# Gather loop of a graph and mixture kernel: in its last 254 tiles each product waits for the tile before it, and four loops of the sort written out

## What is computed

```python
xn = _layernorm(x, axis=-1)
# graph: 100000 edges; edge_row = src, edge_col = dst (nodes), edge_val = weight
gathered = edge_val[:, None] * xn[edge_col]
agg = jax.ops.segment_sum(gathered, edge_row, num_segments=N_NODES)
x = x + einsum('nd,od->no', agg, W) + b + linear_attention(xn)
# then two of eight experts for each node
x = x + ffn(_layernorm(x))
```

## Time and profile before

| | us |
|---|---|
| median of 3 runs | 2421.96 (2420.9 to 2422.66) |
| the profiled execution, its own time | 2401.91 |
| its span, first to last instruction | 2400.1 |
| sort: POOL's indirect DMAs, first to last | 117.2 to 304.4 |
| gather loop: POOL's first gather to the last add | 324.4 to 1656.9 |
| of it tiles 648 to 901, first to last add | 1298.3 to 1656.9 |

### The profile page before, as it was taken

One profiled execution on the slowest core, in us unless ns is written; L12 is line 12 of the kernel. 1 busy time (PEld: TensorE's weight loads), 2 busy tenths in 40 slices (PEclk: granted clock), 3 DMA queues, 4 the chain that ended last, 5 costly groups with the idle time before them and its releaser, 6 DMA issues. The chain is left out here.

```text
span 2400.1 us, 48331 instructions
## 1 busy us (share of the span) xinstructions
PE 1626.9 (68%) x13448; PEld 1218.7 (51%) x13448; DVE 1423.3 (59%) x3495; ACT 1317.3 (55%) x4250; POOL 1388.1 (58%) x1333
## 2 busy tenths in 40 slices
PE   6877435666666566666564444344549999999998
PEld 3565424454544455455452222222347777777776
DVE  7998535555556565555565555556845555555555
ACT  6455335555555555555555555554556565656555
POOL 3688846666666666666666666665404444444443
PEclk8898868888887788888886565655559999999999
DMA  4022144444444443333333333433512223232222
GB/s 147 14 84 75 58 127 136 133 134 136 136 134 131 130 123 101 104 103 102 104 91 90 93 110 116 154 123 98 173 31 44 50 47 50 45 51 47 48 48 32
DMA packets 139656, 225.26 MB, mean 94 GB/s; under 512 B 33398, under 2 KB 94016, under 8 KB 139298
## 3 DMA queue, kind: packets, MB, share of 16 engines
q0 software_dynamic: 67040, 146.22, 23.5%
q1 hardware_dynamic: 66022, 69.75, 9.2%
q10 hardware_dynamic: 6364, 6.40, 0.8%
HBM read 181.40 MB, written 41.82 MB: 93 GB/s over the span
## 5 line engine op out<-in xcount | busy, mean ns | idle before, releaser
L950 POOL DMA_INDIRECT misc<-z_d,consts x902 | 857.3, 950 | 485.6 <-issue 233.5
L1197 DVE SCALAR_TENSOR_TENSOR acc<-ps,consts,acc 128x256 f32 x902 | 433.7, 481 | 543.9 <-remote 418.9
L975 ACT ACTIVATE misc<-rec,misc 128x128 f16<-128x128 f16 x678 | 230.1, 392 | 275.1 <-DVE rec L1057 202.0
L975 ACT ACTIVATE rec<-rec,misc 128x128 f16<-128x128 f16 x674 | 229.4, 392 | 269.8 <-DVE rec L1057 202.2
L1787 ACT ACTIVATE misc<-ps,misc 128x128 f32<-128x128 f32 x840 | 239.5, 367 | 239.2 <-PE ps L1752 165.4
L1828 POOL DMA_INDIRECT out<-misc,pos x105 | 166.1, 1582 | 291.1 <-ACT misc L1852 258.7
L1752 PE MATMUL ps<-misc,big 128*128 128x128 f16 x1680 | 327.5, 220 | 0.0
L1750 PE MATMUL ps<-misc,big 128*128 128x128 f16 x1680 | 327.2, 220 | 0.2
L1751 PE MATMUL ps<-misc,big 128*128 128x128 f16 x1680 | 327.0, 220 | 0.0
L1767 PE MATMUL ps<-big,rec 128*128 x840 | 319.7, 381 | 0.1
L1279 PE MATMUL ps<-misc 128*128 128x256 f16 x565 | 183.3, 324 | 191.3 <-DVE acc L1197 123.6
(11 more groups left out here) (335 smaller groups left out, 3792.5 us busy)
## 6 DMA issues: line engine op xcount, KB each, us to landing
big<-in_w2T SPq DMA_DIRECT2D x60, 256.0 KB
misc<-z_d,consts POOLq DMA_INDIRECT x902
big<-xT_d SPq DMA_DIRECT2D x98, 128.0 KB
big<-in_w1T SPq DMA_DIRECT2D x32, 256.0 KB
tok_d<-misc SPq DMA_DIRECT2D x50, 132.0 KB, 1.9
xT_d<-misc SPq DMA_DIRECT2D x49, 128.0 KB
z_d<-misc SPq DMA_DIRECT2D x49, 128.0 KB
acc<-in_x SPq DMA_DIRECT2D x1, 6144.0 KB
```

The source lines that it names most:

```text
L950: e.indirect_dma_start(out=rows[k], out_offset=None, in_=c.z_d, in_offset=bass.IndirectOffsetOnAxis(ap=idx[u][:, k:k + 1], axis=0)).then_i ...
L975: e.activation(hot[t % HG][:, half, :], same[t % OG], ACT.Copy, scale=near[n // UG % 3][:, t % UG, 1 + half:2 + half]).then_inc(s_hot, 1)
L1197: e.scalar_tensor_tensor(out=rows_of, in0=out_ps[t % BG], scalar=c.gain, in1=rows_of, op0=ALU.mult, op1=ALU.add).then_inc(s_add[k], 1)
```

## The change

In turns from 27 on (tiles 648 to 901) each product waits for the add of the preceding tile instead of every second one for the add five tiles back, and each add waits for its own tile's product instead of every second one for the next tile's. Turns before 27 are as they were. In `rank` the helper `fours` is gone: DVE, ACT, PE and SP have their 28 steps written out, with the same steps and the same waits.

```diff
-def fours(e, steps, body):
-    assert steps % 4 == 0
-    for u in range(4):
-        body(Turn(0, u))
-    with e.Fori(1, steps // 4 - 1) as j:
-        for u in range(4):
-            body(Turn(j, u))
-    for u in range(4):
-        body(Turn(steps // 4 - 1, u, u < 3))
...
-            fours(e, NG, store)
+            for i in range(NG):
+                store(Turn(i // 4, i % 4, i < NG - 1))
...
-            fours(e, NG, hot)
+            for i in range(NG):
+                hot(Turn(i // 4, i % 4, i < NG - 1))
...
-            fours(e, NG, sorting)
+            for i in range(NG):
+                sorting(Turn(i // 4, i % 4, i < NG - 1))
...
                     if B0 <= at < L0 and x == 0 and live(b - 4):
                         add_mix(b - 4)
-                    if t % 2 == 0:
+                    if at >= L0:
+                        e.wait_ge(s_mm[k], q + 1)
+                    elif t % 2 == 0:
                         e.wait_ge(s_mm[k + 1], q + 1)
                     e.scalar_tensor_tensor(out=rows_of, in0=out_ps[t % BG], scalar=c.gain, in1=rows_of,
                                            op0=ALU.mult, op1=ALU.add).then_inc(s_add[k], 1)
...
                 e.wait_ge(s_row[k], 16 * (q + 1))
-                if t % 2 == 0:
+                if j >= L0:
+                    wait(e, s_add[(k - 1) % UG], j * 2 + (t - 1) // UG + 1)
+                elif t % 2 == 0:
                     wait(e, s_add[(k - BG + 1) % UG], j * 2 + (t - BG + 1) // UG + 1)
```

## The result

| | before | after |
|---|---|---|
| median of four runs, us | 2421.44 (2420.9 to 2422.66) | 2477.24 (2472.65 to 2481.34) |
| the profiled execution, its own time, us | 2401.91 | 2481.34 |

The ratio is 1.0229, with a 95% interval of 1.0214 to 1.0244: the changed kernel is slower, by 56 us in the medians. The two profiled executions are 79 us apart: that of before was 20 us under its median, that of the changed kernel 4 us over its own. Where 12 of the 20 us probably lie, the experiments tell.

What follows compares the result with a forecast made beforehand. POOL was taken as nearest to the bound, at 86% of the pace, otherwise waiting for buffers freed late. The serial chain (+60 us) and late signals (13 us) gave +73: 2422 + 73 = 2495 us, range 2447 to 2600.

Steps and rivals of the forecast that it cites:

- The chain: Last 254 tiles: PE and DVE take turns, 1.64 us a tile; 419 us with loads against 358.6, +60 us.
- Load of start columns: DVE's load once in 24 tiles of the gather loop: some 0.4 us over each time, 11 times, 4 us.
- The allowance for late signals: Last 254 tiles: products signalled late to DVE's adds, 1 us in one tile of twenty, 13 us.
- Run-ahead and the late signal: Gather loop before: adds waited 160.2 us in 39 waits, cause open; PE's run-ahead follows in bursts, which the change forbids.
- The base: Whole kernel: 20 us between the profile's 2401.91 us and the median 2421.96 kept; a profiled execution would show 2475.
- Covered work: Last 254 tiles: comparison and weight split, 1.00 us, fit in PE's 1.16 us turn; ACT and POOL cost nothing either.
- POOL's extra wait: Sign in the last 254 tiles: POOL waits 0.3 to 0.4 us beyond its gap at nearly every gather.
- The sort: Sort written out: costed at nothing, as POOL's DMAs set the stage; at most 10.6 us less, or a few more.
- Rival 1: Last 254 tiles: the late signal strikes every tile, 2.85 us each, +366 us, 2788 us; chance 0.11.
- Rival 2: Last 254 tiles: TensorE's clock high, 1.33 us a tile, 2404 us; chance 0.09 with rival 3 and clock mixes.
- Rival 3: Gather loop: run-ahead caused late signals, POOL alone bounds at 1.25 us, 2380 us; chance 0.09 with rival 2 and mixes.

Runs made afterwards that it cites:

- waits_only: The kernel before with only the gather loop's waits of the change, the sort keeping its loops; 2479.49 us, ratio 1.0234.
- own_bank_1: As waits_only, but the six half banks of PSUM of tiles 648 to 901 lie in six banks instead of three; 2479.80 us, ratio 1.0237.
- fill_6: waits_only with six unneeded matmuls behind each product of tiles 648 to 901; 2440.25 us, ratio 1.0132.
- sort_only: The changed kernel with the gather loop's waits of the kernel before, so only the sort is written out; 2420.84 us, ratio 0.9992.
- fill_3: waits_only with three unneeded matmuls behind each product of tiles 648 to 901; 2467.94 us, ratio 1.0248.
- eight_ahead: The kernel before, but in tiles 648 to 901 a gather waits for the product 8 tiles back instead of 12; 2210.71 us, ratio 1.0001.
- own_bank_2, 3 and 5: As own_bank_1, but each product waits for the add two, three or five tiles back; ratios 1.0008, 1.0005 and 1.0010.
- pace_1: The kernel before with one small POOL write behind each gather of tiles 648 to 901; 2213.46 us, ratio 1.0015.
- own_bank_3: As own_bank_1, but each product waits for the add three tiles back; 2408.54 us, ratio 1.0005.

## Why the prediction was right

The forecast was 2495 us (2447 to 2600) and slower at 0.93; 2477 was measured. Step by step:

- **The chain.** Links 0.15 + 0.80 + 0.21 + 0.48 = 1.64 us; measured 0.15, 0.80, 0.20 and 0.48. All four were taken from single places of the old trace and held within 0.01 us. The stretch was forecast at 419 us without lateness and took 419.0: 253 x 1.63 = 412.4, the loads below 3, the late add at 1319.85 (3.54 after the one before it) 1.9, and 1.7 us in rounding and single tiles. That the two agree to the last digit is luck: the forecast's 1.64 was 0.01 a tile too long, and that made room for the 1.9 us of lateness. waits_only and own_bank_1 show that the chain is the whole cause.
- **Load of start columns.** Forecast 0.4 us a time. In the timeline an add after such a load comes 1397.45 - 1395.57 = 1.88 us after the last, 0.25 over 1.63: 3 us in all for the forecast 4. There are ten of them between the first and the last add and not 11, since the first one, at 1296.5 before, lies ahead of the first add.
- **The allowance for late signals, 13 us.** This is the term that was mis-sized, against a measured 2 us in this profile and 5 in waits_only. From the third tile on none was late; the first two cost about (2.43 + 2.88) - 2 x 0.99 = 3.3 us, 1.9 of it behind the first add. Without the allowance the forecast would have been 2482.
- **Run-ahead and the late signal.** The prediction left the cause open and tied the bursts to run-ahead ("That run-ahead is what the change forbids"); one could take from this that run-ahead is to blame. It is not: two, three and five tiles of run-ahead have the same time, and fill_6 had late signals with none. It did no harm to the sum, since the chain was costed by itself.
- **The base.** I kept the 20 us between the profile of before and its median as a constant. It was not one: a profile of 2475 was forecast and 2481.34 came, 4 us over the median and not 20 under it. The add of tile 648 stood at 1298.3 in that profile and at 1310 in those of waits_only and sort_only, in code that is the same. The term of the last 254 tiles was not touched by it: sort_only had 359.6 us there for 358.6.
- **Covered work.** Comparison, weight split, ACT and POOL cost nothing, as said. POOL's extra wait is 0.69 us in front of a gather, its gap of 0.30 included, which is the forecast 0.3 to 0.4.
- **The sort.** Costed at nothing, measured at 0.9992 (0.9983 to 1.0001). The trace's +5 us stood at the limit I had named, and was a difference of executions. The rule of the Trainium skill ("Runtime: NRT & Kernel Launch", "Instruction fetch mechanics"), that a taken branch whose target is not at hand waits for a fetch, bought nothing that these runs can tell: POOL's DMAs set the stage, and DVE had 20 us of slack.
- **Rival 1** (a late signal in every tile) did not come. Its 2.85 us was no tile's time either, but the distance between two releases, of the last gather and of an add, by the signals of two different products; the tiles that were late at the start of a chain took 3.54 us (changed kernel) and 5.00 (waits_only). **Rival 2** (high clock) did not come by itself: 49% busy, and 68% in fill_3, left 0.50; fill_6 showed its time of 1.33 us for a plain tile to be right once the clock is there. **Rival 3** had the right pace for a loop without late signals, and the wrong cause for them.

One thing the prediction did not see: the price of the change hangs on a condition that the kernel does not set. With late signals the loop before needs 359 us for these tiles. Without them eight_ahead, whose time is that of the kernel before (ratio 1.0001), needs 323. The chain has no use of that. By these numbers it would cost 419 - 323 = 96 us where the kernel before takes 2210 us, a ratio of about 1.04. That is an estimate; the changed kernel was not run there.

No version beat the kernel before. Those with run-ahead and POOL unhindered, sort_only, own_bank_2, 3 and 5 and eight_ahead, equal it, pace_1 nearly so (1.0015), and the rest are slower.

## What to carry to other kernels

When a change makes two engines take turns, read each link (release to start, work, end to release) at a place where it is seen alone, and add them up: the sum held here to 0.01 us. A serial chain hides nothing, and this one lost next to nothing to lateness, so compare it with what the overlapped loop would reach at its best, not only with what it reached in one profile. And where a profile is full of waits with no releaser, look at the spread between comparisons before building on their cause: here they held 200 us that came and went with the kernel unchanged.

## What was not expected of the hardware

- The same kernel took 2407 us and 2210 us on one chip in two comparisons, steadily in each. By the profiles of own_bank_3 and eight_ahead, each of which takes what the kernel before took beside it, all of it lies in the gather loop: 1336.6 and 1139.2 us from the first gather to the last add, 197 us apart, as their spans are. In the one adds waited up to 10.6 us for products that were done by the records, in the other no such wait is left. The cause is open.
- PE's late signals come in order and 0.05 us apart (1509.14 to 1509.34 in the kernel before), though the products had ended up to 5.9 us apart; signals of DVE's adds in the same stretch are within 0.01 us of the add's end, in all 134 that the trace records.
- In the row of 1500 to 1600 us PE was 68% busy with three extra matmuls a tile and stayed at the 1.2 GHz level (fill_3); with six the same row shows 2.4 GHz throughout (fill_6), and the rows around it 0.92 to 0.94.
- A semaphore hand-over between DVE and PE took 0.15 us one way and 0.20 the other, tile after tile.
- A POOL write of 40 columns with a semaphore wait of its own can be nearly free behind an indirect DMA: the first added under 0.01 us to the time from gather to gather (1.284 us, for 1.280 in eight_ahead), two added 0.22 and four 0.61.
